# Pacing the edge gathers: from four waits per quad of gathers to two

## The reference, cut to what matters

```python
Q = (h @ Wq).reshape(n, H, HD); K = (h @ Wk).reshape(n, H, HD); V = (h @ Wv).reshape(n, H, HD)
score = jnp.einsum('ehd,ehd->eh', Q[dst], K[src]) / np.sqrt(HD)
score = score + jax.nn.relu(efeat @ W1 + b1) @ W2 + b2
m = jax.ops.segment_max(score, dst, num_segments=n)
ex = jnp.exp(score - m[dst])
denom = jax.ops.segment_sum(ex, dst, num_segments=n)
alpha = ex / denom[dst]
out = jax.ops.segment_sum(alpha[:, :, None] * V[src], dst, num_segments=n)
```

## Time and profile before

| | |
|---|---|
| median of 3 runs | 3356.6 us |
| lowest and highest | 3353.1 and 3365.98 us |
| the profiled execution | 3331.86 us, its span 3330.0 us |
| mean granted TensorE clock of it | 0.91 |
| gathers, first and last start | 254.0 and 1644.8 us |

### The profile page before, as it was taken

The page is one execution under the profiler, slowest core; times in us unless marked ns, Lnnn a source line. Parts: engine busy times, 40 slices in busy tenths (PEclk is TensorE's granted clock), DMA queues, the critical chain, the costliest instruction groups (busy, mean ns, idle before and its releaser), DMA issues. The chain is left out here.

```text
span 3330.0 us, 62642 instructions
## 1 busy us (share of the span) xinstructions
PE 2574.1 (77%) x18415; PEld 1880.2 (56%) x18415; DVE 2312.8 (69%) x4036; ACT 1275.3 (38%) x2919; POOL 1464.6 (44%) x1363
## 2 busy tenths in 40 slices
PE   0885888888888888888845399957999999977048
PEld 0442555555555555555544255646999889976035
DVE  8543777777777777777746377667999898955701
ACT  0331544454545544454511011136454444543011
POOL 4685666666666666666523317034000000024251
PEclk9996999999999999999977599979999999988579
DMA  6226888888888888888722433210000000011040
GB/s 160 64 76 182 234 237 235 231 240 234 236 235 238 234 235 233 236 240 241 198 45 80 108 114 94 75 49 21 9 11 11 11 11 9 11 42 46 27 131 26
DMA packets 252155, 428.59 MB, mean 129 GB/s; under 512 B 58711, under 2 KB 162496, under 8 KB 251875
## 3 DMA queue, kind: packets, MB, share of 16 engines
q0 software_dynamic: 91920, 235.61, 26.5%
q1 hardware_dynamic: 156736, 185.86, 19.2%
q10 hardware_dynamic: 3344, 5.11, 0.4%
HBM read 508.04 MB, written 155.53 MB: 199 GB/s over the span
## 5 line engine op out<-in xcount | busy, mean ns | idle before, releaser
L1111 POOL DMA_INDIRECT edge_kv<-scratch_kv,edge_idx x784 | 889.8, 1135 | 477.6 <-issue 205.9
L1455 PE MATMUL edge_ps_o<-edge_vals,edge_onehot 128*128 128x264 f32 x1568 | 451.7, 412 | 108.5 <-ACT edge_rows L1320 98.2
L1136 DVE TENSOR_TENSOR edge_prod<-edge_ps_q,edge_kv 128x512 f32<-128x512 f32 x392 | 259.5, 688 | 358.8 <-PE edge_ps_q L1370 247.9
L2893 PE MATMUL msg_ps_o<-all_fp,msg_at 125*123 125x256 bf16 x3375 | 437.6, 278 | 20.2 <-ACT msg_at L2946 16.8
L1455 PEld LDWEIGHTS edge_ps_o<-edge_vals,edge_onehot 128*128 128x128 f32 x1568 | 265.5, 194 | 275.4 <-ACT edge_rows L1320 189.8
L1320 ACT ACTIVATE edge_rows<-edge_ps_o 128x264 f32<-128x264 f32 x784 | 291.8, 393 | 294.0 <-PE edge_ps_o L1455 239.9
L2893 PEld LDWEIGHTS msg_ps_o<-all_fp,msg_at 125*123 125x123 bf16 x3375 | 373.9, 138 | 26.6 <-ACT msg_at L2946 19.8
L1245 ACT ACTIVATE edge_hid<-edge_ps_h,edge_b 128x512 f32<-128x512 f32 x392 | 248.9, 688 | 205.0 <-PE edge_ps_h L1339 140.8
L1370 PE MATMUL edge_ps_q<-edge_qw,edge_slots 128*128 128x256 bf16 x2352 | 297.8, 277 | 32.1 <-DMA edge_qw<-scratch_qc 18.8
L1370 PEld LDWEIGHTS edge_ps_q<-edge_qw,edge_slots 128*128 128x128 bf16 x2352 | 217.6, 99 | 149.8 <-issue 109.3
L2918 POOL TENSOR_TENSOR msg_x<-msg_x,msg_b 125x256 f32<-125x256 f32 x25 | 29.2, 1167 | 616.4 <-PE msg_ps_n L2869 616.4
(11 more groups left out here) (525 smaller groups left out, 4310.4 us busy)
## 6 DMA issues: line engine op xcount, KB each, us to landing
edge_qw<-scratch_qc SPq DMA_DIRECT2D x980, 192.0 KB
scratch_part<-edge_rows SPq DMA_DIRECT2D x196, 396.0 KB
scratch_part<-edge_rows SPq DMA_DIRECT2D x196, 132.0 KB
edge_ef<-in_edge_t_dram SPq DMA_DIRECT2D x98, 256.0 KB
edge_sgb<-scratch_seg SPq DMA_DIRECT2D x98, 256.0 KB
ffn_w<-in_L_ffn_w_dram SPq DMA_DIRECT2D x18, 1024.0 KB
edge_kv<-scratch_kv,edge_idx POOLq DMA_INDIRECT x784
scratch_kv<-tab_kvrow SPq DMA_DIRECT2D x25, 250.0 KB
```

The costliest lines, as they stand in the source:

```text
L1111: pool.indirect_dma_start(kv[p][:, t, :], None, K.kv_d, bass.IndirectOffsetOnAxis(ap=idx[p][:, t:t + 1], axis=0)).then_inc(rows_in[p][q], 16)
L1136: dve.tensor_tensor(prod[:, 2 * h:2 * h + 2, :], ps_q[h][:].rearrange("e (t d) -> e t d", t=2), kv[pp][:, s * QT + 2 * h:s * QT + 2 * h + ...
L1455: pe.matmul(ps_o[t % 2][:, 0:RW], onehot[q % 2][:, t, :], vals[q % 2][:, t, :], start=True, stop=True).then_inc(out_done, 1)
L2893: m = pe.matmul(ps_o[gl % 3][0:GR, 0:D], at[gl % 3][:, h, :], K.fp[:, h, k, :], start=h == 0 and k == 0, stop=h == NT - 1 and k == 2)
```

## The change

POOL's second gather of a quad no longer waits for `out_done` but for the first half of the queries of quad W + 6, for which the third waited. The third and the fourth wait for nothing of their own and follow the second. The first still waits for the values. Only POOL's program changes; all lines after it move up by one.

```diff
@@ -1102,10 +1102,9 @@
                     pool.wait_ge(idx_ready, G + 1)
                     for q in range(NQ):
                         W = (G - 2) * NQ + q
-                        paced = ((vals_ready, W + 1), (out_done, QT * (W + 1)),
-                                 (q_done, 2 * (W + AHEAD + 1) + 1), (q_done, 2 * (W + AHEAD + 1) + 2))
+                        paced = ((vals_ready, W + 1), (q_done, 2 * (W + AHEAD + 1) + 1))
                         for t in range(q * QT, (q + 1) * QT):
-                            if not isinstance(G, int) or G > 1:
+                            if t % QT < 2 and (not isinstance(G, int) or G > 1):
                                 pool.wait_ge(*paced[t % QT])
                                 pool.nop(nofuse=True)
                             pool.indirect_dma_start(kv[p][:, t, :], None, K.kv_d,
```

## The result

The changed kernel takes **3417.9 us** (median of 4, 3413.6 to 3427.6), the kernel before beside it 3361.3 us (4 runs). The ratio is 1.0172, 95% interval 1.0141 to 1.0202, so the change costs 57 us. The prediction was 3396 us, range 3328 to 3470, chance of slower 0.58. The sign and the range held; the 39 us forecast are two thirds of the 57 that came.

The account below looks back on a forecast made before the run. The prediction took a stall of about 3 us per 28.1 us group, behind a long gather run with full DMA engines, as on the path. It added 47 x 0.84 = 39 us to 3356.6: 3396 us, range 3328 to 3470.

Parts of the forecast that it names:

- What bounds the stage: Edge attention: a long run of gathers with full DMA engines stalls PE, DVE and ACT, about 3 us per 28.1 us group.
- It adds no work; dropping waits costs 0: POOL's gathers: the two dropped waits and their no-ops cost nothing beyond any gather's 0.30 us, so 0.
- The release of the first half a place earlier, and no wait between (3,1) and (0,1): POOL's order: first half of queries releases (q,1), not (q,2); (3,2) and (3,3) follow unheld, at about 1.25 us.
- In sum one gather of 256 KB per group moves into the stall, 0.84 us: Gather run's end: one gather per group moves from the quiet stretch into full DMA engines; 47 x 0.84 = 39 us.
- The load theory: Gathers in the stall: their data is what costs, so each group pays for what is moved into it.
- DVE's "remote" waits were to be 109 us: Sign on DVE: its waits ended by "remote" would rise from 74.6 to about 109 us over as many groups.
- two groups were to take 57.8 us: Sign in the edge attention: two groups would take 56.1 + 1.7 = 57.8 us.
- the DMA share was to be above 1.00 for longer: Sign on the DMA engines: share in a group's last quarter higher than 1.00 for longer than before.
- the late release was not to come before POOL's run ends: Sign at the stall: the late release coming before POOL's run of gathers ends would show the prediction wrong.
- The second rival: Stall lasts until POOL rests, after (0,0): +4.4 us x 47 = 207 us, 3563 us, or 3460 with half; chance 0.16.
- The first rival, no change: Moved gather's data flows after the stall, so gathers only trade places in a queue: 3357 us; chance 0.28.
- The third rival, faster: Quieter stretch after the stall lets SP and PE run ahead: 0.75 us per group, 35 us, so 3321 us; chance 0.14.

Follow-up runs that it names:

- the C waits: Waits on next quad's second-tile `out_done`: in place of the change's second wait, or as the before-kernel's fourth without its second; 3158.7 and 3158.0 us beside 3159.2.
- the change with the memset: The changed kernel plus a 1.29 us scratch memset on POOL ahead of gather (3,2): 3154.6 beside 3159.2 us, again 3155.4 beside 3160.2.

## Why the prediction was right, and where it wasn't

**What bounds the stage: held.** The stall at the end of the run of gathers was the place. Every kernel that is over 1% slower than before on that kind of chip is so by longer stalls. One reading was loose: in the group shown DVE saw its news 3.5 us after the record, but ACT only 2.8 us after that of `edge_ps_m`, which ends at 1023.55 (1026.30 in the earlier trace rows).

**"It adds no work; dropping waits costs 0": held.** A gather has 0.30 us ahead of it and 1141 ns of its own, as before.

**The release of the first half a place earlier, and no wait between (3,1) and (0,1): held.** The slots at 1.25 us are there, and so is the 4 us wait ahead of (0,1): a mean of 4.07 us over the groups. The wait for `edge_ps_o` is gone.

**"In sum one gather of 256 KB per group moves into the stall, 0.84 us": this step failed, and it is the term that was mis-sized.** It gave 39 us in place of 57. That this put the time into the range is luck in part: the sign and the place were read from the trace, but the loss came by another way. I had priced it as load, the same in each of 47 groups. The load theory then wanted 3370 us with the wait for the second half gone, at least 3400 with that wait kept as the only one beside the wait for the values, and at most 3360 with the values alone; they took 3406, 3370.5 and 3631. In place of 0.84 us in each group stand 6.4 us (34.6 - 28.2) in 10 of 42 and -0.4 us in the others. Four of my own signs were against the step: DVE's "remote" waits were to be 109 us and were 73.1; two groups were to take 57.8 us, where the mean is 58.9 and the median 56.7; the DMA share was to be above 1.00 for longer, while it is 0.78 in the stall; and the late release was not to come before POOL's run ends, while in the group that goes well both halves came at 1030.03, with four gathers of the run still to be issued.

**The second rival, "the stall lasts until POOL rests", with chance 0.16, comes nearest to what the runs show.** I had POOL's first rest behind (0,0) in every group, so 4.4 us x 47. The extra length was about right for a group that misses its rest, 6 us. What I didn't see is that the wait at (3,1) is itself a rest, and in three groups of four a sufficient one. The trace of before had the parts: in it POOL's waits for the two halves stand one behind the other, the one ahead of (3,2) with 0.56 us of idleness and the one ahead of (3,3) with 1.27. Over the 42 groups the first is 0.30 to 0.66 us in 40, and the second 0.75 to 1.71 in those. I took these slots as fixed and moved the gathers down a place. I should have asked which of the two waits gives the rest in which the news comes, since the change removes just that one.

**The first rival, no change,** had beside it the rule of the Trainium skill ("SBUF — State Buffer", section "SBUF: two separate sides") that a DMA and a compute instruction can't slow each other. On the second kind of chip the runs agree with it: at DMA share 0.95 no wait ends by "remote". On the first kind they don't bear it out as the whole story, since a program with other waits and the same instructions otherwise took 1.7% longer. That isn't a slower instruction, though: a gather took 1.14 us and a product 0.69 us as before. It is late news, of which that section says nothing. The Trainium skill, in "Perfetto Trace Analysis", section "Summary: the profiler window per engine type", says that the end of a TensorE record is an estimate and that the way of a semaphore isn't in the profile. The trace agrees: a record that ends at 969.6 and its consumer at 976.73.

**The third rival, faster,** came true in a small part: the groups that rest are 0.4 us shorter. It isn't enough.

**Shown, argued, open.** Shown: the loss sits in single groups; removing the wait for the second half alone makes it, and removing the `out_done` wait makes none (1.0005); with as many waits it depends on which event POOL waits for; and over 84 groups of two executions of the change POOL's rest tells every long group from every other, with no overlap. In the kernel without `out_done` the same short rest does no harm; a longer one follows in each of its 19 cases. The theory of the load as it was priced is refuted by three of its forecasts (3370, 3400 to 3430 and 3280 to 3360 us against 3406, 3370.5 and 3631). Argued from this, not shown by a run of its own: that it is POOL's rest as such, whatever gives it, that lets the news through. The run meant for that, with a pause by POOL's own work, fell on chips where nothing is held. Open: what holds the news, POOL's issuing or the packets that it makes, so that the data of a run of gathers may still have a part in it; why the rest at (3,1) is short in some groups, since in both groups shown POOL reached it 2.7 to 2.8 us behind PE's first query matmul; whether the C waits or the pause beat the kernel before on a chip of the first kind; and why chips are of two kinds.

## What to carry to other kernels

A wait that looks redundant for correctness can be what makes an engine pause, and a pause is worth something only if its event is still to come when the engine gets there: before removing or moving one, read for each wait how often and how long it really waits, and what news is pending then. Of two events for the same wait in a long run of gathers the later was the better one here (3370.5 in place of 3417.9 us), since it is seldom met already. And compare the distribution over repetitions of a stage, not the mean: "+1.2 us per group" was 6 us in a quarter of them and a gain in the rest.

## What was not expected of the hardware

- News of PE was held for 7 us and more: `edge_ps_m` recorded as done at 969.6, seen at 976.73. The news of `edge_ps_m` came through mostly in rests of POOL, 0.4 to 1.3 us into them. The pauses of 0.30 us between gathers let little through: in the group shown the second half of the queries, 5 us after its record, and not what came behind it.
- SP was slow in the same stage: of its records between 400 and 1600 us, two that follow one another started 0.6 to 0.8 us apart 711 times in 5370 before, 683 in 5141 after, and 45 in 5457 on a chip of the second kind (the change with the memset).
- Chips differed by 6% for the same program: 3356 and 3160 us. Most of it is in the stage of the gathers: 1391 us from the first to the last for the kernel before on the one, 1217 to 1232 for the three kernels traced with whole rows on the other (the kernel before has no trace there), with the clock from 400 to 1400 us at 0.96 and 1.00 and the DMA engines at 234 and 267 GB/s (on the other for the change with the memset). The change costs 57 us on the one. On the other the nearest that was run, the change with the memset, costs nothing.
